# The last cross attention: another order of SyncE's stores and slanted reads, and of TensorE's projections

## What is computed

```python
q = heads(x @ Wq);  k = heads(ctx_t @ Wk);  v = heads(ctx_t @ Wv)
sim = einsum('bihd,bjhd->bhij', q, k) * SCALE
dist = clip(arange(TEXT)[None, :] - arange(nq)[:, None], -16, 16) + 16
sim = sim + einsum('bihd,ijd->bhij', q, rel_k[dist]) * SCALE
attn = softmax(sim)
out = einsum('bhij,bjhd->bihd', attn, v) + einsum('bhij,ijd->bihd', attn, rel_v[dist])
out = out + stream(Wk_ip, Wv_ip, ctx_i) * (tanh(alpha) + 1)   # a softmax of its own
out = out + stream(Wk_ap, Wv_ap, ctx_a) * (tanh(beta) + 1)    # a softmax of its own
return out.reshape(b, nq, INNER) @ Wo + bo
```

## Time and profile before

| | us |
|---|---|
| median of 3 runs | 2693.28 (2693.03 to 2693.37) |
| the profiled execution, its own time | 2707.29 |
| its span, first to last instruction | 2705.6 |
| mean granted TensorE clock | 0.929 |

### The profile page before, as it was taken

How to read it: one execution, slowest core, us unless ns; L and a number is a source line. 1 busy time by engine, 2 the same in 40 slices (tenths; PEclk the granted TensorE clock), 3 DMA queues, 4 the chain that set the end, 5 groups by cost and what they waited for, 6 DMA issues and landing times. The chain is left out here.

```text
span 2705.6 us, 46196 instructions
## 1 busy us (share of the span) xinstructions
PE 2334.2 (86%) x16760; PEld 1734.1 (64%) x16760; DVE 1454.7 (54%) x3024; ACT 1145.9 (42%) x2827; POOL 806.2 (30%) x945
## 2 busy tenths in 40 slices
PE   7979869999797889869999979999689987888765
PEld 5867655666475887645666558887456566767652
DVE  5767401222565786721222446666566674666648
ACT  4468522222576735411222233333574653433335
POOL 4656240112354531140111102122110102444355
PEclk9999779999899899879999989999799998999878
DMA  5000452113200300060211320000200004555620
GB/s 180 2 1 2 167 192 73 47 45 143 103 2 1 97 1 2 27 246 8 106 45 44 148 83 2 1 1 1 94 1 1 1 15 147 175 166 164 189 63 32
DMA packets 119126, 190.65 MB, mean 70 GB/s; under 512 B 60599, under 2 KB 88375, under 8 KB 113914
## 3 DMA queue, kind: packets, MB, share of 16 engines
q1 hardware_dynamic: 109786, 160.65, 18.1%
q0 software_dynamic: 9120, 27.04, 2.8%
HBM read 110.39 MB, written 77.27 MB: 69 GB/s over the span
## 5 line engine op out<-in xcount | busy, mean ns | idle before, releaser
L2108 POOL TENSOR_TENSOR l2a_Pn<-l2a_Pn,l2a_rden 128x1024 f32<-128x1024 f32 x32 | 60.1, 1897 | 295.8 <-DVE l2a_rden L2350 295.8
L1678 DVE TENSOR_TENSOR l1f_work<-l1f_work,l1f_psU 128x512 f32<-128x512 f32 x55 | 37.8, 687 | 195.7 <-PE l1f_psU L1426 167.1
L1442 PE MATMUL l1f_psY<-l1f_W,l1f_hT 128*128 (+1 forms) x440 | 106.1, 385 | 25.0 <-ACT l1f_hT L1539 25.0
L1533 ACT ACTIVATE l1f_work<-l1f_psG 128x512 f32<-128x512 f32 x55 | 32.8, 597 | 210.1 <-PE l1f_psG L1419 185.8
L1351 POOL DMA_INDIRECT results_by_token<-l1f_rows_in_out,l1f_dest x39 | 37.2, 955 | 266.0 <-DVE l1f_rows_in_out L1689 266.0
L3934 DVE TENSOR_TENSOR_SCAN l3x_cum<-l3x_segments_begin,l3x_Pn 128x1024 f32<-128x1024 f32 x32 | 78.6, 2458 | 66.1 <-ACT l3x_Pn L3794 66.1
L1442 PEld LDWEIGHTS l1f_psY<-l1f_W,l1f_hT 128*128 128x128 f32 x440 | 81.4, 193 | 42.0 <-ACT l1f_hT L1539 25.9
L1351 POOL DMA_INDIRECT results_by_token<-l0f_rows_in_out,l0f_dest x39 | 37.2, 955 | 230.9 <-DVE l0f_rows_in_out L1689 230.9
L3713 PE MATMUL l3x_psT<-ident,l3x_Pn 128*128 128x128 f32 x256 | 43.7, 326 | 68.6 <-POOL l3x_Pn L3863 68.3
L1678 DVE TENSOR_TENSOR l0f_work<-l0f_work,l0f_psU 128x512 f32<-128x512 f32 x39 | 26.8, 688 | 128.2 <-PE l0f_psU L1426 122.1
L885 ACT ACTIVATE l1a_att_Pn<-l1a_att_psS,l1a_att_nmx 128x128 f32<-128x128 f32 x256 | 91.8, 418 | 1.7 <-DVE l1a_att_nmx L1004 1.7
(11 more groups left out here) (797 smaller groups left out, 7122.2 us busy)
## 6 DMA issues: line engine op xcount, KB each, us to landing
relative_rows<-l3x_ext SPq DMA_DIRECT2D x32, 516.0 KB, 3.7
l1f_W<-in_l1f_w SPq DMA_DIRECT2D x9, 1536.0 KB, 6.5
l0f_W<-in_l0f_w SPq DMA_DIRECT2D x8, 1536.0 KB
cumulative_rows<-l3x_cum SPq DMA_DIRECT2D x32, 384.0 KB, 4.9
rows_by_expert<-zeros SPq DMA_DIRECT2D x2, 5011.5 KB, 26.8
l3x_K<-keys SPq DMA_DIRECT2D x16, 512.0 KB, 5.0
l3x_rel<-relative_rows SPq DMA_DIRECT2D x32, 231.0 KB, 3.0
values<-l1f_W SPq DMA_DIRECT2D x11, 512.0 KB
```

Source lines behind the costliest of these rows:

```text
L1442: ins = nc.tensor.matmul(psY[:, 0:D], hT[n % 2][:, j * P:(j + 1) * P], weights(n, 2 * DC * F + j * D, D), start=(j == 0), stop=(j == FC - 1))
L1533: nc.scalar.activation(sg[n % 2], psG[:, :], ACT.Silu).then_inc(sg_ready, 1)
L1678: nc.vector.tensor_tensor(h[n % 2], sg[n % 2], psU[:, :], ALU.mult).then_inc(h_ready, 1)
L2108: nc.gpsimd.tensor_tensor(part, part, rden[b % 2][:, 8 * u:8 * u + 8].unsqueeze(2).to_broadcast([P, 8, P]), ALU.mult)\
```

## The change

SyncE: `near_weights` is split into `store_sums` and `load_near`, `relative_scores` into `store_relative` and `load_relative`. In one iteration SyncE now stores the sums of unit it+1, loads the relative scores of unit it+3 (stored one iteration earlier), loads keys or values, stores the relative scores of unit it+4, and then loads the near values of unit it+1.

TensorE: `project` moves from the iteration's end to behind `scores`, `project_out` from there to the end. ScalarE's `take_q` follows (behind `take_pT`). `project`'s wait for the addition is for one batch less, `project_out` waits for one more `take_q`.

GpSimd: the weights of unit it+1 come before the near values of unit it. VectorE: `add` moves to the iteration's end, behind the row statistics and the feed-forward's maxima.

```diff
     def results_before(it):
-        return min(max(0, (it - 1) // 2), NB)
+        return min(max(0, (it - 2) // 2), NB)
...
         for it in range(-4, UN):
+            if 0 <= it + 1 < UN:
+                store_sums(it + 1)
+            if 0 <= it + 3 < UN:
+                load_relative(it + 3)
             if it % 2 == 0 and it + 4 < UN:
                 load_keys((it + 4) // 2)
             if it % 2 and it >= -1 and it + 1 < UN:
                 load_values((it + 1) // 2)
+            if it + 4 < UN:
+                store_relative(it + 4)
             if it == -1:
                 sp.wait_ge(edge_stored, 32)
             if 0 <= it + 1 < UN:
-                near_weights(it + 1)
-            if it + 4 < UN:
-                relative_scores(it + 4)
+                load_near(it + 1)
...
-            pe.wait_ge(q_taken, min(it + 8, UN))
+            pe.wait_ge(q_taken, min(it + 9, UN))
...
                 scores(it + 2)
-            if it % 2 and it >= 3:
-                project_out((it - 3) // 2, it)
+            if it + 8 < UN:
+                project(it + 8, it)
             if 0 <= it - 1 < UN:
                 transpose_near(it - 1)
             if 0 <= it + 4 < UN:
                 relative_keys(it + 4, it)
             if 0 <= it - 1 < UN:
                 weigh(it - 1)
-            if it + 8 < UN:
-                project(it + 8, it)
+            if it % 2 and it >= 3:
+                project_out((it - 3) // 2, it)
...
         for it in range(-1, UN):
+            if it + 1 < UN:
+                weights(it + 1)
             if it >= 0:
                 near_values(it)
-            if it + 1 < UN:
-                weights(it + 1)
...
-            if it % 2 and it >= 3:
-                add((it - 3) // 2)
             if it % 2 == 0 and it >= 4:
                 row_stats((it - 4) // 2)
...
+            if it % 2 and it >= 3:
+                add((it - 3) // 2)
```

More of the change, by code:

```diff
@@ L3611, in load_values, with store_sums @@
                 sp.dma_start(V[b % 2][SEG0[s]:SEG0[s] + SEG[s], :], G.VD[r0:r0 + SEG[s], :]).then_inc(v_loaded[b % 2], 16)
-        def near_weights(n):
+        def store_sums(n):
             i = n % 2
@@ L3617, in near_weights, with load_near @@
             sp.dma_start(G.CD[i, EDGE:].rearrange("(r e) -> r e", e=HH * P), cum[i][0:ROWS, :]).then_inc(cum_stored[i], 16)
+        def load_near(n):
+            i = n % 2
             sp.wait_ge(cum_stored[i], 16 * (n // 2 + 1))
@@ L3622, in near_weights, with store_relative @@
             sp.dma_start(near[i][0:ROWS, :].rearrange("p (h d) -> p h d", h=HH), slanted).then_inc(near_loaded[i], 16)
-        def relative_scores(n):
+        def store_relative(n):
             i = n % 2
@@ L3629, in relative_scores, with load_relative @@
             sp.dma_start(G.RD[i].rearrange("(r e) -> r e", e=HH * EXT), ext[i][0:ROWS, :]).then_inc(ext_stored[i], 16)
+        def load_relative(n):
+            i = n % 2
             sp.wait_ge(ext_stored[i], 16 * (n // 2 + 1))
@@ L3815, in _ @@
                 take_pT(it)
+            if it + 8 < UN:
+                take_q(it + 8)
             if 0 <= it - 1 < UN:
@@ L3821, in _ @@
                 take_o(it - 1)
-            if it + 8 < UN:
-                take_q(it + 8)
             if 0 <= it + 2 < UN:
```

## The result

| | us |
|---|---|
| before, median of 4 runs | 2693.32 (2693.03 to 2697.85) |
| after, median of 4 runs | 2630.76 (2625.56 to 2632.76) |
| ratio after to before | 0.9761, 95% interval 0.9742 to 0.9779 |
| the profiled execution after, its own time | 2629.06 (span 2627.3, mean clock 0.939) |

The changed kernel is faster by 62.6 us. In its code the steps stand at other lines: transposes L3723 (T), scores L3714, queries' projection ("proj") L3681, near transposes L3730, relative keys L3701, weighing L3745 and L3749, output rows ("out") L3758; weights L3873 on GpSimd; scan L3944 and addition L3959 on VectorE; on SyncE sums' store L3617, relative load L3639, relative store L3632, near load L3625.

A forecast was written before the change was run, and what follows sets the result against it. Bound: SyncE's serial chain of two round trips, 21.45 us a pair. Terms 11.5 + 49.0 + 7 - 1.3 = 66 us; 2707.3 less 66 is 2641.3, less 14.0 gives 2627 us, range 2619 to 2635.

The forecast's parts named there:

- the loop through the addition: Addition, scan, weights, transposes, output rows across VectorE, GpSimd and TensorE: 16.2 us a pair, hidden under TensorE's 17.0.
- The two gaps: TensorE's idle times ahead of the near transposes (ScalarE's 1.0 us copy) and the queries' projection (0.46 us, addition), both removed.
- (1): Start of the stage, T(0) to T(4): T(4) at 2300.4 against 2311.88, 11.5 us less.
- (2): T(4) to T(26), 11 pairs of units: from 21.45 to 17.0 us a pair, 49.0 us less.
- (3): T(26) to T(28), at the feed-forward weights: 27 us instead of 34, 7 less, bounds 2 and 9.
- (4): Last units, output rows no longer filling the wait for the copy: 1.3 us lost, bounds 0 and 3.7.
- A: The addition's loop becomes the bound, GpSimd's weights meeting VectorE's scan: 18.2 us a pair, 2640 us; chance 0.16.
- B: SyncE still sets the pace as the sums' round trip grows: 19.2 us a pair, 2651 us; chance 0.13.
- C: The near load behind the extended scores closes a two-unit ring, deciding from 12.5 us landings: 2710 us; chance 0.03.
- D: TensorE waits as long for GpSimd instead: about 21 us a pair, 2680 to 2693 us; chance 0.02.
- SyncE could turn in 6 to 7 us: SyncE's queue per unit, with about 5.4 us of round trip and 0.4 of issue left.
- free pace: VectorE's pace read from two scans at the start: 7.5 us a unit, 15.0 a pair.

The follow-up runs named there:

- e1: The kernel before with SyncE's new order alone, all other engines keeping theirs: 2610.23 us against 2646.49 (0.9852), 18.27 us a pair.
- e2: The kernel after with SyncE's old order, all other engines keeping the new one: 2643.34 us (0.9987 against the kernel before), 21.71 us a pair.
- e6: The kernel after with the output rows' products done twice: 2674.86 us (0.9936 against the kernel before), 20.39 us a pair.
- e4: The kernel before with the new orders of SyncE and GpSimd, the other engines keeping theirs: 2598.69 us (0.9828), 18.06 us a pair.
- e10: The kernel after with feed-forward maxima by TensorE in unit 28, W2's load and the weights' scaling and rounding later, no clip: 2633.78 us (0.9748).
- after again: The kernel after, unchanged, profiled in another session: 16.93 us a pair, T(26) to T(28) 29.03 us.
- e9: The kernel after with the near load directly behind its own store again: 2651.05 us (0.9812 against the kernel before), 18.31 us a pair.
- e11: The kernel after with the relative load directly behind its own store again: 2665.73 us (0.9863 against the kernel before), 18.39 us a pair.
- e8: The kernel after with the feed-forward weights' maxima over partitions by TensorE transposes and VectorE, not GpSimd's all-reduce: 2625.40 us (0.9741 against the kernel before).

## Why the prediction held

**What bounded it: right.** It said that one serial chain of SyncE's two round trips set 21.45 us a pair. e1 and e2 show it from both sides.

**What is next: right.** TensorE at 17.0 a pair; measured 16.93, T to T 10.18 and 6.73 where it said 10.3 and 6.7, and TensorE busy 184.36 of 186.26 us; e6 agrees. Close behind, as it said, is the loop through the addition: 0.9 us to spare, where it had 0.8. The two gaps that it said the order of TensorE removes are the 1.13 us between e4 and after.

**The terms**, predicted and measured: (1) the start 11.5 and 11.39. (2) T(4) to T(26) 49.0 and 49.7. (3) T(26) to T(28) 7 and 6.4 (5.0 in the second profile of after). (4) The last units, 1.3 lost: from T(28) 24.98 + 98.73 against 24.73 + 98.97, so nothing was lost; the charge was too high by 1.3, within its bounds. Sum 66 and 67.5 (67.3 to T(31)).

**The rivals.** A did not come about: the weights took 2.20 us, as its "against" said; the stretched scan of e10 shows that the collision is there for a placement that asks for it. For B, SyncE's waits for the sums are 11.6 us by 10 times, 1.2 on average where it named 3 as the most, though the longest is 5.2; the share of the DMA engines rose to 0.78, not 0.72. C: the near load lands in 5.2 us in the median and 7.0 at most, far from 12.5. D: the pair is 16.93, not 21.

**Where it was off.** First, the profiled execution of before was 14.0 us longer than the median. I carried this as if it belonged to a profiled execution. Of after it is 1.7 us under its median: 2629.06 us where the sum in the profiled execution gave 2641.3. T(0), which I held at 2267.64, came at 2256.89: 10.75 us of the 78 between the two spans lie ahead of the stage, in parts that the change doesn't touch. Since the 14.0 was taken off again, the forecast was in effect the median less 66 and was not hurt; that the forecast of the profiled execution was 12 us too long does not show in it. Of the gain, 67.3 us were seen in the stage and 62.6 in the medians; in the session of "after again" the medians differ by 67.5. I take this gap for the spread of the runs; no run was made to show it.

Second, the sentence that SyncE could turn in 6 to 7 us kept 5.4 us as what is left of a round trip, whatever stands ahead of it. In the new order the store of sums lands in 3.3 us. SyncE waits 83.1 of 180 us for the scan and 13.5 for the extended scores, so that its own turn comes to about 4 us (an estimate: the remaining 83.4 us by 21 units). The 6 to 7 was too long there, and the same way of counting was too short in e9 and e11, which missed by 1.4 us a pair: a landing has to be counted with what stands ahead of it.

Third, the near load's landing was counted at 2.3 us and is 5.2 in the median; the prediction's own upper value of 6.0, which adds the whole store ahead of it, was the right way to count, and it stays hidden.

Fourth, VectorE's "free pace" of 7.5 us a unit has 1.12 us of waiting for ScalarE in it; the start came out right (11.39) because the new start runs with the same wait.

Fifth, the reduction of (3), kept at 13.2 us, took 14.2, and (3) came out at 6.4 instead of 7.

## What to carry to other kernels

Where one queue stores something, waits for it and reads it back, order its issues so that each load stands behind other issues or a whole turn behind its store; count a transfer's landing with what is issued just ahead of it, never by its size alone. Then size the engine that is next by a unit in which it already runs without gaps; here that gave the new pace to 0.1 us. Reordering the other engines shows nothing as long as the queue sets the pace (e2), and is worth 1.1 us a pair once it doesn't (e4).

## What the runs showed of the hardware that I had not expected

- The same 384 KB store lands in 3.3, 4.9 or 5.9 us, and the same 96 KB load in 2.2 or 5.2, by what stands ahead of it.
- The kernel before took 2646.49 us in one session and 2692.04 and 2702.62 in two others. The traces of e1 to e4 are shorter by this much ahead of the stage, whose own times repeat within 1.5 us in the two profiles of the kernel after. Half of it lies in one wait: in the first experts' layer VectorE waits 49.3 to 51.7 us for rows scattered to DRAM and read back (`rows_by_expert`) in e1 to e4, and 72.4 to 76.1 in the others. The other half lies at the same work of the second experts' layer, where TensorE comes from its counting products (L1394) to the first experts' product (L1402) in 83 us in e1 to e4 and in 105 to 112 in the others. Why these scattered transfers land sooner in one session stays open.
- A reduction over partitions on GpSimd that is recorded with 0.39 us gives its result 6.4 us after its last input and holds GpSimd for 14.2; e8's exchange over TensorE, from 2495.34 to 2496.87, gives the same values in 1.5.
- A scan of 2.29 us on VectorE took 5.15 beside GpSimd's scaling of 128x2048 (e10). By the Trainium skill ("GPSIMD Engine Reference", section "Key points") VectorE instructions with two SBUF inputs contend with GpSimd; the scan is one, and the trace agrees.
- In e8 TensorE waits 2.10 us for a copy, and its granted clock is 0.57 in the 3.5 us behind that wait and 0.62 in the output rows (from 2496.93 to 2502.57). In the kernel after the wait at this place is 1.83 us, and the clock behind it 0.56. In e10 waits of 1.38 and 1.20 us, 3.4 us apart, left it at 1.00 (from 2487.16 to 2503.70).
